# Preparing the expert weights' half-precision parts in the first attention layer, and a new order for the stacked queries and keys

## The reference

```python
x = x + L0_attn(layernorm(x))        # 16 heads of 16, full, weights alpha*sign(W)
x = x + L0_xattn(layernorm(x), ctx)  # one head
x = x + L0_ffn(layernorm(x))         # inner 1024, quantised
x = x + L1_attn(layernorm(x))        # 4 causal heads, 12 with a window of 64
x = x + L1_xattn(layernorm(x), ctx)  # 16 heads
x = x + L1_ffn(layernorm(x))         # shared expert and top 2 of 8 experts
...
# L1_ffn, for each token (inner width 512):
shared = silu(xt @ sg_w.T) * (xt @ su_w.T) @ sd_w.T
probs  = sigmoid(xt @ router_w.T + routing_bias)
topk_p, topk_idx = top_k(probs, 2)   # normalised to sum 1
routed = sum over the two experts of topk_p * (silu(xt @ wg.T) * (xt @ wu.T)) @ wd.T
return shared + routed
```

## Time and profile before

| | us |
|---|---|
| median of 3 runs | 2143.51 (2140.32 to 2156.59) |
| profiled execution, its own time | 2145.49 |
| its span | 2143.4 |
| layer 0's self-attention, in the span | 0 to 575 |
| cross-attention and FFN of layer 0 | 575 to 848 |
| layer 1's self-attention | 848 to 1350 |
| last cross-attention | 1350 to 1583 |
| experts: routing stretch | 1583 to 1762 |
| experts: block stretch and end | 1762 to 2143 |

### The profile page before, as it was taken

How to read it: one execution, slowest core, us unless ns; L and a number is a source line. 1 busy time by engine, 2 the same in 40 slices (tenths; PEclk the granted TensorE clock), 3 DMA queues, 4 the chain that set the end, 5 groups by cost and what they waited for, 6 DMA issues and landing times. The chain is left out here.

```text
span 2143.4 us, 36053 instructions
## 1 busy us (share of the span) xinstructions
PE 1688.7 (79%) x12334; PEld 859.7 (40%) x12350; DVE 1316.8 (61%) x3599; ACT 1118.9 (52%) x1534; POOL 979.4 (46%) x987
## 2 busy tenths in 40 slices
PE   4888888888688887477777776577747779999997
PEld 2122222222245455123333333344424446666664
DVE  2666777777157897246666664455448865555555
ACT  2366676676445796245555554255446634444442
POOL 3144554541347630456777766255327751212222
PEclk8588999999789999669999988699968889999999
DMA  5331334330040000333333320322224432222216
GB/s 102 65 58 36 62 65 65 61 50 1 5 122 1 1 1 5 52 53 51 54 53 53 58 41 11 84 53 58 47 88 133 132 126 54 61 62 62 58 41 245
DMA packets 114435, 130.26 MB, mean 61 GB/s; under 512 B 22108, under 2 KB 98908, under 8 KB 114108
## 3 DMA queue, kind: packets, MB, share of 16 engines
q1 hardware_dynamic: 107780, 109.74, 25.0%
q0 software_dynamic: 6480, 18.23, 2.2%
HBM read 79.25 MB, written 47.55 MB: 59 GB/s over the span
## 5 line engine op out<-in xcount | busy, mean ns | idle before, releaser
L653 ACT ACTIVATE at_pexp<-ps 128x1024 f32<-128x1024 f32 (+3 forms) x480 | 385.8, 826 | 194.3 <-PE ps L890 193.1
L714 DVE TENSOR_REDUCE at_mx<-ps 128x1 f32<-128x512 f32 x512 | 324.2, 684 | 146.9 <-PE ps L897 144.9
L897 PE MATMUL ps<-at_ks,at_qs 48*128 48x512 f16 (+3 forms) x1024 | 288.7, 357 | 91.6 <-DVE at_mx L714 42.4
L161 PE MATMUL ps<-mo_wall,mo_xt 128*128 x1704 | 301.5, 327 | 1.0 <-DVE mo_xt L2540 0.5
L890 PE MATMUL ps<-at_qs,at_ks 50*128 50x512 f16 (+4 forms) x1024 | 249.7, 341 | 27.7 <-DMA at_qs<-at_mhl 23.1
L950 PE MATMUL ps<-at_pexp,at_vaug 128*32 128x512 f32 (+4 forms) x2048 | 223.4, 529 | 13.9 <-issue 11.2
L161 PEld LDWEIGHTS ps<-mo_wall,mo_xt 128*128 128x128 f16 x1704 | 161.2, 98 | 94.6 <-issue 3.5
L2304 POOL DMA_INDIRECT mo_yd<-mo_xn,mo_idu x71 | 68.1, 959 | 275.8 <-DVE mo_xn L2561 267.0
L716 DVE CUSTOM_DVE_ANT_0 at_junk<-ps,at_lmask 128x192 bf16<-128x192 f32 x384 | 115.5, 353 | 78.7 <-PE ps L897 77.5
L897 PEld LDWEIGHTS ps<-at_ks,at_qs 48*128 48x128 f16 x1024 | 75.6, 98 | 206.1 <-DVE at_mx L714 122.6
L2364 ACT ACTIVATE mo_sg<-ps 128x512 f32<-128x512 f32 x71 | 42.4, 597 | 186.9 <-PE ps L161 186.9
(11 more groups left out here) (396 smaller groups left out, 3853.2 us busy)
## 6 DMA issues: line engine op xcount, KB each, us to landing
at_qs<-at_scratch SPq DMA_DIRECT2D x96, 128.0 KB, 7.2
at_ks<-at_scratch SPq DMA_DIRECT2D x96, 128.0 KB, 7.8
mo_xw<-mo_xs SPq DMA_DIRECT2D x71, 136.0 KB, 2.4
at_scratch<-at_qkh SPq DMA_DIRECT2D x64, 128.0 KB, 1.8
at_scratch<-at_qkl SPq DMA_DIRECT2D x64, 128.0 KB, 1.8
mo_wall<-mo_yd SPq DMA_DIRECT2D x16, 512.0 KB, 10.8
x_qs<-x_queries SPq DMA_DIRECT2D x48, 128.0 KB
mo_stage<-in_m_gate SPq DMA_DIRECT2D x9, 512.0 KB, 3.9
```

What stands on the lines that cost most here:

```text
L161: last = nc.tensor.matmul(out, lhs, rhs, start=(n == 0), stop=(n == len(terms) - 1))
L653: last = act.activation(columns(pexp[:, U % 2, hh], at, n, stride, width), columns(banks(r, ST[S % 2], 2), at, n, stride, width), ACT.Exp, ...
L714: last = ve.reduce_max(out, score, AX.X)
L897: return nc.tensor.matmul(banks(r, MX[i % 2])[:, piece.at:piece.at + piece.n], qs[rows, (n // 2) % 2, h // 2, piece.idx * P:(piece.idx + 1 ...
```

## The change

1. Layer 0's self-attention also splits the expert weights. After the 12 pieces of the linear weights come 54 more, 6 for each of the 9 sets, of [128, 512] as before. `CHUNK_AT` gives 9 slots a batch at which SyncE loads a piece; POOL scales it and makes both halves one slot later (after its other steps of that slot); four slots after the load SyncE saves both halves (256 KB) to a DRAM buffer `moe_weights`. A load waits until the piece before last is done, a high half until the save of the piece before last has landed.
2. The experts' phase loads the finished halves: 1.5 MB for the shared expert at its start and 1.5 MB for each expert when a further batch is turned. ACT's and DVE's splits, the buffer `stage` and the table `SPLIT` are gone.
3. Queries and keys are saved in the order in which they are stacked: three saves for each group (high twice, low once), and four reads a batch of 48 partitions with 8 KB each instead of twelve of 16 partitions with 1 KB runs. The last cross-attention does the same with its queries.
4. Of the shared expert's four low halves of a batch, numbers 1 and 3 are made by DVE, 0 and 2 stay on POOL; one semaphore for each parity.
5. The slots in `ROUTE` and `SHARED` are others. The last scatter of the last batch, for one, moves from slot 247 to 256, which is behind the first low half of the last shared batch of this stretch (slot 253).

```diff
+CHUNK_AT = (1, 3, 5, 14, 15, 17, 28, 29, 31)
+CHUNK_DO = (1, 1, 1, 4)
...
-        scratch = nc.dram_tensor(f"{tag}_scratch", (nb, 2, P, 4, T), F16, kind="Internal").ap()
+        scratch = nc.dram_tensor(f"{tag}_scratch", (nb, 2, 2, 3 * DH, NP_, T), F16, kind="Internal").ap()
...
+        MOE_CHUNKS = 6 * (E_ + 1)
+        CHUNKS = LIN_CHUNKS + MOE_CHUNKS
+        def chunk_at(i):
+            return CHUNK_AT[i % len(CHUNK_AT)] + K * (i // len(CHUNK_AT))
...
             def save(b, m):
-                to = scratch[b] if b < nb else r.x1_queries[b - nb]
+                of_k, par = divmod(m, 2)
+                to = scratch[b, of_k, par] if b < nb else r.x1_queries[b - nb, par]
                 sp.wait_ge(qkh_ready, qk_before(b) + m + 1)
-                sp.dma_start(to[0, :, m, :], qkh[:, m, :]).then_inc(saved, 16)
+                for rep in (0, 1 + of_k):
+                    sp.dma_start(to[rep * DH:(rep + 1) * DH].rearrange("d i t -> i d t"), qkh[:, m, :]).then_inc(saved, 16)
                 sp.wait_ge(qkl_ready, qk_before(b) + m + 1)
-                sp.dma_start(to[1, :, m, :], qkl[:, m, :]).then_inc(saved, 16)
+                rep = 2 - of_k
+                sp.dma_start(to[rep * DH:(rep + 1) * DH].rearrange("d i t -> i d t"), qkl[:, m, :]).then_inc(saved, 16)
...
                 for par in range(2):
-                    for rep, (qpart, kpart) in enumerate(((0, 0), (0, 1), (1, 0))):
-                        rows = slice(64 * par + 16 * rep, 64 * par + 16 * rep + 16)
-                        sp.dma_start(qs[rows, p], scratch[b, qpart, :, par, :].rearrange("(i d) t -> d i t", d=DH)).then_inc(stacked, 16)
-                        sp.dma_start(ks[rows, p], scratch[b, kpart, :, 2 + par, :].rearrange("(i d) t -> d i t", d=DH)).then_inc(stacked, 16)
+                    rows = slice(64 * par, 64 * par + 3 * DH)
+                    for of_k, to in enumerate((qs, ks)):
+                        sp.dma_start(to[rows, p].rearrange("p i t -> p (i t)"), scratch[b, of_k, par].rearrange("p i t -> p (i t)")).then_inc(stacked, 16)
...
+            def keep_halves(j):
+                s, n, half = moe_chunk(j)
+                sp.wait_ge(lin_done, 2 * (LIN_CHUNKS + j + 1))
+                at = n * NW + half * WCHUNK
+                sp.dma_start(r.moe_weights[s, :, :, at:at + WCHUNK], whalves[:, j % 2]).then_inc(halves_out[j % 2], 16)
...
-                if binary and t >= 0 and t % (K // 2) == 4 and t // (K // 2) < LIN_CHUNKS:
-                    load_lin(t // (K // 2))
+                if binary:
+                    for i in chunks(t):
+                        load_lin(i)
+                    for i in chunks(t - CHUNK_DO[3]):
+                        if i >= LIN_CHUNKS:
+                            keep_halves(i - LIN_CHUNKS)
...
+            def scale_chunk(i):
+                w = wstage[:, i % 2, :]
                 pool.wait_ge(lin_in[i % 2], 16 * (i // 2 + 1))
-                w = wstage[:, i % 2, :]
                 pool.tensor_tensor(w, w, unit[:].broadcast_to([P, WCHUNK]), ALU.mult).then_inc(lin_step, 1)
+            def chunk_high(i):
+                j = i - LIN_CHUNKS
+                if j >= 2:
+                    pool.wait_ge(halves_out[j % 2], 16 * (j // 2))
                 pool.wait_ge(lin_step, i + 1)
-                pool.tensor_copy(r.wh[:, c, at:at + WCHUNK], w).then_inc(lin_done, 1)
+                pool.tensor_copy(halves_of(i)[0], wstage[:, i % 2, :]).then_inc(lin_done, 1)
+            def chunk_low(i):
+                high, low = halves_of(i)
                 pool.wait_ge(lin_done, 2 * i + 1)
-                pool.tensor_tensor(r.wl[:, c, at:at + WCHUNK], w, r.wh[:, c, at:at + WCHUNK], ALU.subtract).then_inc(lin_done, 1)
+                pool.tensor_tensor(low, wstage[:, i % 2, :], high, ALU.subtract).then_inc(lin_done, 1)
...
-ROUTE = {"STAT": -22, "RSTD": -17, "APPLY": -10, "HIGH": -10, "LOW": 2, "TURN": (-9, 6), "XT": (-3, 12), "LG": 6, "LOGITS": 17, "SIG": 16,
-         "CHOOSE": 20, "RANK": 18, "SLOTS": 27, "SCAT": (28, 30, 33, 49, 49, 49, 50, 51)}
+ROUTE = {"STAT": -22, "RSTD": -21, "APPLY": -15, "HIGH": -9, "LOW": -13, "TURN": (-15, -6), "XT": (-8, 11), "LG": -2, "LOGITS": 12, "SIG": 12,
+         "CHOOSE": 15, "RANK": 12, "SLOTS": 23, "SCAT": (29, 32, 35, 47, 47, 47, 54, 60)}
...
-SHARED = {"GU": (11, 12, 41, 45), "SQ": (22, 33, 48, 50), "H": (26, 42, 49, 56), "HH": (38, 47, 48, 62), "HL": (43, 50, 66, 70), "PROJ": (64, 66),
-          "UPD": (77, 97)}
+SHARED = {"GU": (11, 13, 33, 37), "SQ": (29, 43, 52, 56), "H": (36, 43, 52, 57), "HH": (45, 53, 59, 65), "HL": (43, 52, 62, 66), "PROJ": (67, 69),
+          "UPD": (71, 90)}
...
-SPLIT = {"LOAD": (-105, -83, -71), "WHI": (-58, -42, -34), "WLO": (-42, -28, -19)}
...
-            for t in range(START, END):
-                for s, n in due(t, "LOAD"):
-                    load_weights(s, n)
-
+            sp.dma_start(sh[:].rearrange("p q n w -> p (q n w)"), r.moe_weights[0].rearrange("p q w -> p (q w)")).then_inc(sh_in, 16)
+            for e in range(E):
+                sp.wait_ge(xt_ready, 2 * (e + 1))
+                sp.dma_start(wall[:, e * EW:(e + 1) * EW], r.moe_weights[1 + e].rearrange("p q w -> p (q w)")).then_inc(wall_in, 16)
...
                 for b, i in due(t, "HL"):
-                    low_hidden(b, i)
+                    if i % 2 == 0:
+                        low_hidden(b, i)
...
+            def low_hidden(b, i):
+                n = b * NI + i
+                ve.wait_ge(hh_ready, n + 1)
+                ve.tensor_tensor(hl[:, i, :], h[:, pair(n), :], hh[:, i, :], ALU.subtract).then_inc(hl_ready[i % 2], 1)
...
             def project(b, half):
-                pe.wait_ge(hl_ready, (b + 1) * NI)
+                for i in range(2):
+                    pe.wait_ge(hl_ready[i], (b + 1) * NI // 2)
```

More of the change, by code:

```diff
@@ L289, in attention_phase @@
             wstage = sb("wstage", [P, 2, WCHUNK])
+            whalves = sb("whalves", [P, 2, 2, WCHUNK], F16)
+            halves_out = [sem(f"halves_out{i}") for i in range(2)]
             x_in = [sem(f"x_in{b}") for b in range(nb)]
@@ L354, in attention_phase, with chunks, moe_chunk @@
         LIN_CHUNKS = NC * NLIN // WCHUNK
+        MOE_CHUNKS = 6 * (E_ + 1)
+        CHUNKS = LIN_CHUNKS + MOE_CHUNKS
+        def chunk_at(i):
+            return CHUNK_AT[i % len(CHUNK_AT)] + K * (i // len(CHUNK_AT))
+        def chunks(t):
+            return [i for i in range(CHUNKS) if chunk_at(i) == t]
+        def moe_chunk(j):
+            return j // 6, j % 6 // 2, j % 2
         def main_at(t):
@@ L583, in _ @@
                     normalise((t - place["NORM"]) // K)
-                if binary and t >= K // 2 and t % (K // 2) == 4 and t // (K // 2) - 1 < LIN_CHUNKS:
-                    split_lin(t // (K // 2) - 1)
+                if binary:
+                    for i in chunks(t - CHUNK_DO[0]):
+                        scale_chunk(i)
+                    for i in chunks(t - CHUNK_DO[1]):
+                        chunk_high(i)
+                    for i in chunks(t - CHUNK_DO[2]):
+                        chunk_low(i)
         @block.scalar
@@ L1741, in save, with to @@
                 sp.wait_ge(q_ready, NC * (f + 1))
-                sp.dma_start(r.x1_queries[p, 0], qh[:]).then_inc(saved, 16)
+                def to(par, rep):
+                    return r.x1_queries[p, par, rep * DH:(rep + 1) * DH].rearrange("d i t -> i d t")
+                for par in range(2):
+                    for rep in range(2):
+                        sp.dma_start(to(par, rep), qh[:, par, :]).then_inc(saved, 16)
                 sp.wait_ge(ql_ready, f + 1)
-                sp.dma_start(r.x1_queries[p, 1], ql[:]).then_inc(saved, 16)
+                for par in range(2):
+                    sp.dma_start(to(par, 2), ql[:, par, :]).then_inc(saved, 16)
             def stack(b):
@@ L1755, in stack @@
                 if b >= AHEAD:
-                    sp.wait_ge(saved, 32 * (b - AHEAD + 1))
-                for rep, part in enumerate((0, 0, 1)):
-                    for par in range(2):
-                        at = 64 * par + 16 * rep
-                        sp.dma_start(qs[at:at + 16, p], r.x1_queries[p, part][:, par, :].rearrange("(i d) t -> d i t", d=DH)).then_inc(stacked[p], 16)
+                    sp.wait_ge(saved, 96 * (b - AHEAD + 1))
+                for par in range(2):
+                    sp.dma_start(qs[64 * par:64 * par + 3 * DH, p].rearrange("p i t -> p (i t)"), r.x1_queries[p, par].rearrange("p i t -> p (i t)")).then_inc(stacked[p], 16)
             def rows(b):
@@ L2311, in _ @@
         def _(act):
-            def split(s, n):
-                act.wait_ge(w_in[n], 16 * (s + 1))
-                act.activation(part_of(s, 0)[:, n * NW:(n + 1) * NW], stage[:, n, :], ACT.Copy, scale=WS).then_inc(w_hi, 1)
             def high(b):
@@ L2358, in _ @@
                     sigmoid(b)
-                for s, n in due(t, "WHI"):
-                    split(s, n)
             def block_squash(k):
@@ L2517, in _ @@
```

(12 more changed lines are left out.)

76 lines of the change are left out of this document (37 added, 39 removed).

## The result

The changed kernel takes **2177.73 us** (2168.06 to 2184.67), the kernel before in the same session 2142.87: ratio 1.0152, 95% interval [1.0116, 1.0188]. Forecast were 2128 and a range up to 2163, so it was wrong in size and in sign. The profiled execution took 2175.54 us (span 2173.8).

The account below looks back on a forecast made before the run. Layer 0 was taken as bound by POOL's hand-over of the maxima's split to PE, routing next by POOL, blocks by PE. +28 - 16 - 28 = -16 gave a median of 2128 us, range 2096 to 2163.

Parts of the forecast that it names:

- Part 1, layer 0: Layer 0's self-attention: expert-weight pieces make POOL 4 us late at each of 7 batch changes, +28 us (+10 to +70).
- late by 2.6: Layer 0 batch change: POOL stands 6.3 us at best for the first load, against 3.7 us of room.
- rival C: Layer 0 chains up: POOL hands over maxima later and later, PE loses clock; 10 us a batch, 2171 us; chance 0.18.
- the saves' third part: Query and key saves: the third save, issued before the low half is there, adds 0.4 us of queue.
- Part 2, the stacked order: Bare stacking reads at three places get shorter: -7.5, -6 and -2.5 us; bounds nothing to -20 for all three.
- The first read: Start of layer 0: the 1.5 MB stacking read takes 9.1 us instead of 16.9, -7.5 us.
- The two other waits: PE's waits before the first maxima of layer 1 and the last cross-attention: -6 and -2.5 us.
- Part 3, routing: Routing stretch of the experts' phase: -18 us with POOL as next bound, start -6, end -4.
- my end of -35: Routing stretch: far end of the -18 us step, PE's 92 us plus the same idle of a tenth.
- The start: Start of routing: first statistics no longer wait behind two splits of the shared expert, -6 us.
- The end (-4): End of routing: padding writes start some 10 us sooner, but the last scatter stands behind a low half; -4 us.
- The possible quarrel of DVE's low halves with POOL: Routing stretch: DVE's 12 subtractions and POOL's reads could shut each other out, 15 us more of DVE.

Follow-up runs that it names:

- 16 engines: Changed kernel with weight columns permuted so each query/key save writes its 128 rows in one dimension: 2159.70 us, 1.0109.
- nine pieces clear of the stack: Changed kernel with only the places of the nine pieces a batch moved, away from the stack transfers, saves as in the change: 2144.14 us, 0.9992.
- the order alone: Kernel before with only the stacked order of queries and keys (three saves, four reads, all three places): 2136.59 us, 0.9985.
- the version of 2121.9 us: Changed kernel with eight pieces a batch, placed clear of the stack, and saves writing 128 rows in one dimension: 2121.90 us, 0.9915.

## Why the prediction was wrong

**Part 1, layer 0 (+28, came +47.5): the failed step, with the sign.** The place, the engine and the wait that would show it were right: six pieces and two additions in 26.6 us of room, PE waiting for POOL's split. Mis-sized was the time for which POOL stands for loads: 6.3 us "at best" ("late by 2.6"), plus "I add 1.4 us". At the five batch changes it stood 12.3 us on average, 4.6 more. Half of that (2.3) is the landing of the first piece's load, which I took at 2.7 us "since the uncontended landing, 2.7, is the one seen wherever no stack is in flight". I had just put that load behind the rows, the saves and the load of x; it took 5.0 us on average and up to 6.9, the median that the earlier trace rows already showed. The third piece's load behind the stack gives 1.6 (a wait of 3.0 us on average, 1.7 to 3.9, instead of 1.4 for all three), and the first one's later issue the rest. The count was wrong too: not 7 batch changes by 4 us, but five intervals by 9.2 us. So 6.8 us a batch over seven, above the 6.3 from which the prediction's rival C decides. C came true, at its foot, and with most of the mechanism it names: transfers caught at the stack, two buffers, a lower clock. "Later and later" did not come, since PE's six long waits are 8.9, 8.9, 10.1, 10.2, 5.9 and 8.8 us.

I gave 0.4 us to the saves' third part. Rows of the change show two high saves in 1.27 us and the low one in 0.56, with 16 engines 0.91 and 0.45: SyncE itself is slower in issuing them. They also land later (3.4 us for 1.9 above), and a load behind them does (6.9 for 4.3). I had counted that at the two starts alone and not in the loop. With nine pieces clear of the stack the other form was worth 10 us of loop (506.7 to 496.9), where by the rule I had estimated 2 in all. The Trainium skill, "DMA: Bandwidth & Descriptors", section "Why a DMA increments its semaphore by 16 and not by 1", gives such a save 8 engines and the other form 16; the runs agree with its direction (the landings above), and no row shows the engines themselves.

**Part 2, the stacked order (-16, came -6.7 by PE's waits, -4.5 by the stretches).** The first read was to save 7.5 and saved 3.4, in the order alone 3.2. I took 9.1 us for 1.5 MB from one big read over 128 partitions; the four reads of 48 partitions land in 8.1 and 9.7 us each in the median (the twelve: 7.2 and 7.8 each), and PE's wait fell from 13.44 to 10.01 us only. The two other waits fell by 2.3 and 1.0 instead of 6 and 2.5. The lower bound, nothing, was the nearer end.

**Part 3, routing (-28, came -19).** Steady -12 for -18. Slots came 16.0 us apart, as forecast at the upper end ("15 to 16"); the -18 was worked out over 138 us, and the 123.7 us between the slots would have lost 16 of it. But POOL was not the bound that I took it for: it is busy 74.5 of 111 us, where the forecast said "POOL's idle time almost gone". In the new slots the place of the last two scatters held the batches; moved, they give 101.1 us, within my end of -35. The start came as forecast (-6) and 3 more behind it; the same stretch was 216.8 to 225.0 us in ten traces, so a hit to the microsecond is luck. The end (-4) came +1.7. The padding writes start 3.0 us after the last slots instead of 13.3, the 10 us sooner that I had forecast, but the last scatter holds the first block's rows as I had named it, and by more than I gave it. Where it is moved, the shared expert's low half on DVE holds the block for as long. The possible quarrel of DVE's low halves with POOL cost next to nothing: DVE's twelve take 0.68 us in the median and 0.88 at most, POOL's twelve 1.15 and 1.17 at most.

**Not foreseen:** layer 1's loop, +5.6. With the same code for layer 1 the loop was 408.6 us at a granted clock of 0.86 (stack order alone) and 412.7 at 0.84 (the change), each over its own loop. Over all 18 traces it was 406.1 to 408.6 us in the four with 0.86 or more and 408.2 to 413.5 in the others. So a lower clock goes with a longer loop; why the clock was lower there is open.

Between the forecast of -16 and the +30.4 of the traces lie 46.4 us: 19.5 in layer 0's loop, 11.5 in the three stretches of the stack, 8.7 in routing, 5.6 in layer 1's loop and 1.1 in the blocks.

## What to carry to other kernels

When work is put on an engine with free time, its gap at the tightest hand-over has to hold the work *and* the landing of its transfers; take for the landing the value of a transfer issued behind or beside the others on that queue, not the shortest one seen. With two buffers a late save holds the engine as a late load does, so removing the loads alone showed little (521.6 of 533.1 us). Place such transfers by the time at which they are issued, ahead of the big read or a full read's length behind it: here that alone turned 1.0152 into 0.9992. The plain form of the saves made it 0.9942, eight pieces a batch for nine 0.9915, and the scatters' slots 0.9826.

## What the runs showed of the hardware

A 256 KB transfer with a median landing of 2.9 us took 12.1 us when it was issued 0.5 us after the last of four reads of 384 KB, 12.7 in the version of 2121.9 us, and 10.1 for a save issued 0.5 us behind, without sharing any data with them. In the same trace as the 12.7, the load issued 0.7 us ahead of the reads was in use 7.5 us later, without a wait. The Trainium skill, "DMA: Bandwidth & Descriptors", section "Queues, rings and completion order", says that each DMA engine takes up descriptors in the order of its ring; by that the load's are taken up behind the stack's, and these rows agree. When it lands the section does not say; here it was 12 us after its issue.

A save of 128 KB that regroups 128 rows as 8 by 16 kept SyncE 0.57 us in the median, for high and for low halves (the change), the same bytes in one row order 0.43 and 0.32 (the same kernel with 16 engines).

Subtractions of 128x512 on DVE and on POOL in the same stretch hardly slowed each other: 0.68 us in the median and 0.88 at most on DVE, 1.15 and 1.17 on POOL.
